# Graph attention kernel: edge steps of 128 instead of 256, softmax over 20 tiles instead of 16

## What is computed

```python
enh = xn + 0.1 * query_emb
Q, K, V = enh @ Wq + bq, enh @ Wk + bk, enh @ Wv + bv      # (N, 4 heads, 64)
mod_k  = K[src] + 0.2 * rel_w[edge_type]
scores = einsum('ehd,ehd->eh', Q[dst], mod_k) / 8
ex     = exp(scores - segment_max(scores, dst)[dst])
w      = ex / segment_sum(ex, dst)[dst]
agg    = segment_sum(w * V[src], dst)
out    = layernorm(agg @ Wo + bo + xn)                       # then the mix and the experts
```

## Time and profile before

| what | us |
|---|---|
| median of 3 runs (lowest, highest) | 1203.07 (1202.24, 1210.01) |
| the profiled execution, its own time | 1205.97 |
| span of its instructions | 1204.2 |
| busy, all stages: TensorE / VectorE / ScalarE / GpSimd | 1019.1 / 909.2 / 814.2 / 802.1 |

### The profile page before, as it was taken

One profiled execution on the slowest core, in us unless ns is written; L12 is line 12 of the kernel. 1 busy time (PEld: TensorE's weight loads), 2 busy tenths in 40 slices (PEclk: granted clock), 3 DMA queues, 4 the chain that ended last, 5 costly groups with the idle time before them and its releaser, 6 DMA issues. The chain is left out here.

```text
span 1204.2 us, 26894 instructions
## 1 busy us (share of the span) xinstructions
PE 1019.1 (85%) x6959; PEld 778.4 (65%) x6960; DVE 909.2 (76%) x1999; ACT 814.2 (68%) x2902; POOL 802.1 (67%) x873
## 2 busy tenths in 40 slices
PE   4899966888888888888888888878996489999993
PEld 3677744565565556555556565556895478999993
DVE  5777547999998999999999999985996823333331
ACT  3344410489888888898988889863675466766662
POOL 3667657777777777777777777712983347666662
PEclk9899975699998999999999999998997689999997
DMA  8333438888888888888888888876325724444445
GB/s 240 114 122 113 141 105 234 240 248 234 240 240 241 243 239 238 243 242 241 246 243 239 247 244 244 242 242 227 111 71 177 237 53 72 69 70 65 70 66 133
DMA packets 130432, 220.56 MB, mean 183 GB/s; under 512 B 24772, under 2 KB 89452, under 8 KB 129992
## 3 DMA queue, kind: packets, MB, share of 16 engines
q0 software_dynamic: 48832, 138.49, 42.9%
q1 hardware_dynamic: 81480, 80.63, 21.5%
HBM read 188.00 MB, written 34.25 MB: 185 GB/s over the span
## 5 line engine op out<-in xcount | busy, mean ns | idle before, releaser
L668 POOL DMA_INDIRECT KV<-kv,ixs x464 | 471.7, 1017 | 151.5 <-issue 110.9
L684 ACT ACTIVATE KV<-KV,WS 128x65 f32<-128x65 f32 x1728 | 437.2, 336 | 40.7 <-issue 40.6
L811 PE MATMUL ps_o<-KV,PM 128*128 128x260 f32 x928 | 255.5, 399 | 49.1 <-DVE PM L929 31.4
L785 PE MATMUL ps_qe<-Q,PT 128*128 x1392 | 209.6, 288 | 21.8 <-DVE PT L897 12.9
L811 PEld LDWEIGHTS ps_o<-KV,PM 128*128 128x128 f32 x928 | 160.4, 193 | 91.5 <-issue 73.0
L785 PEld LDWEIGHTS ps_qe<-Q,PT 128*128 128x128 bf16 x1392 | 122.4, 100 | 77.3 <-issue 46.5
L918 DVE TENSOR_TENSOR KV<-KV,ps_qe 128x512 f32<-128x512 f32 x232 | 149.5, 674 | 0.2
L911 DVE TENSOR_TENSOR KV<-KV,ps_u 128x1024 f32<-128x1024 f32 x116 | 140.0, 1207 | 12.8 <-DMA KV<-kv,ixs 12.5
L924 DVE TENSOR_REDUCE S<-KV 128x16 f32<-128x1024 f32 x116 | 138.7, 1196 | 1.1
L1705 DVE TENSOR_TENSOR YG<-ps_y,KV 128x256 f32<-128x256 f32 x56 | 23.8, 425 | 140.8 <-PE ps_y L1678 140.8
L1589 POOL DMA_INDIRECT acc<-YG,DX x56 | 88.7, 1583 | 61.3 <-issue 36.9
(11 more groups left out here) (306 smaller groups left out, 1610.5 us busy)
## 6 DMA issues: line engine op xcount, KB each, us to landing
dlb<-dl_rows SPq DMA_DIRECT2D x116, 128.0 KB
tyb<-ty_rows SPq DMA_DIRECT2D x116, 64.0 KB
KV<-kv,ixs POOLq DMA_INDIRECT x464
kv<-kvb SPq DMA_DIRECT2D x25, 258.0 KB, 2.5
xs_rows<-xs SPq DMA_DIRECT2D x25, 256.0 KB, 2.5
KV<-xs_rows SPq DMA_DIRECT2D x10, 640.0 KB, 9.8
Q<-in_f_W_dram SPq DMA_DIRECT2D x8, 512.0 KB, 6.0
KV<-in_f_W_dram SPq DMA_DIRECT2D x8, 512.0 KB, 6.0
```

The source lines that it names most:

```text
L668: pool.indirect_dma_start(kv[:, c % KR, n, :], None, d["kv"], bass.IndirectOffsetOnAxis(ap=T["ixs"][:, c % KR, n:n + 1], axis=0)).then_inc ...
L684: m = a.activation(part, part, ACT.Copy, scale=W[:, c % 2, s * H + h:s * H + h + 1])
L785: m = pe.matmul(T["ps_qe"][:, p % 3, k, :], T["PT"][:, h, (p % 2 * 2 + k) * P:(p % 2 * 2 + k + 1) * P], T["Q3"][:, bass.ds(at + n * C, C)] ...
L811: m = pe.matmul(ps_o[:, bass.ds(bank, A)], PM[:, p // 2 % 2, p % 2 * 2 + k, :], kv[:, c % KR, 2 * x + k, C:KVW], start=False, stop=True, s ...
```

## The change

Steps become one tile: `TE` = 128, ET = 416, 440 steps of one tile each. Chunks become 20 tiles, 5 groups: 22 chunks, 110 groups. The ring of gathered tiles is one ring of 48 tiles (`RING`), and the sums lag the scores by `LAG` = 9 groups; each engine has one loop over x = 0..118 (`NX` = 119). GpSimd reads its indices in `SRC` itself. Every tile now has its own clear and its own copy of the sums: TensorE loads 4 values instead of 2 in each of its three loads per group, ScalarE makes its two loads of 2 values twice per group. VectorE weighs the last tile of every odd group (`by_vector`), and in the last 9 groups three of four. In the projection the list of steps is made with 4 columns instead of 2 (4 gathers of edges instead of 2, 4 counts over 416 entries instead of 2 over 208). The areas of later stages within the ring are placed anew. The diff, cut:

```diff
-TE = 2 * P
+TE = P
-SC = 2
+SC = 4
-CP = 8
-NCH = NS // CP
-CG = 2 * CP // G
-CB_ = 2 * CP
-KR = 3
+CB_ = 20
+NCH = NS // CB_
+CG = CB_ // G
+NG = NS // G
+RING = 48
+LAG = 9
...
+    NX = NG + LAG
+    def by_vector(g):
+        if g >= NG - LAG:
+            return ((1, 1), (2, 2))
+        return ((3, 1),) if g % 2 else ()
...
-            sp.wait_ge(s_pw, (NCH - 2) * CP)
+            sp.wait_ge(s_pw, NS - RING + VB_TILES)
             sp.dma_start(T["VB"], d["kv"][:, C:KVW]...)
...
+            for t in range(NS):                                   # GpSimd
+                g = t // G
+                wait(pool, s_pw, t - RING + 1)
+                if t % G == 0:
+                    wait(pool, s_ku, g - AHEAD + 1)
+                pool.indirect_dma_start(kv[:, t % RING, :], None, d["kv"],
+                                        bass.IndirectOffsetOnAxis(ap=T["SRC"][:, t:t + 1], axis=0))...
...
+            for x in range(NX):                                   # ScalarE
+                c, j = x // CG - 1, x % CG
+                g = x - LAG
+                softmax, summed = 0 <= c < NCH, g >= 0
+                for k in range(G):
+                    t = g * G + k
+                    if summed:
+                        if k % 2 == 0:
+                            at, bank = before(max(t - 1, 0))
+                        if k in by_scalar(g):
+                            weigh(t)
+                        if t >= 2:
+                            copy_sums(t - 1, at[k % 2], bank[k % 2])
+                    if softmax and j == 1 and k == 1:
+                        ends(c)
+                if softmax and j == 2:
+                    exponents(c)
+                if softmax and j == 3:
+                    weights(c)
...
             def rows(G_):                                         # TensorE
-                return load_values(nc, mybir.EngineType.PE, T["qRow"][0:1, 2 * G_:2 * G_ + 2], (NT - 1) * 3 * C)
+                return load_values(nc, mybir.EngineType.PE, T["qRow"][0:1, G * G_:G * G_ + G], (NT - 1) * 3 * C)
...
+                if summed:
+                    own = banks("own_bank", g * G, G)
+                    after = banks("next_bank", max(g * G - 1, 0), G)
+                    shift = 1 if g == 0 else 0
+                def add(k):
+                    t = g * G + k
+                    if summed:
+                        if t >= 2:
+                            clear(t - 1, after[k - shift])
+                        aggregate(t, own[k])
...
+                if scored:
+                    queries(2 * G_, at[0:2])
+                add(0)
+                add(1)
+                if scored:
+                    relations(G_)
+                if softmax and j == 3:
+                    turn_weights(c)
+                if scored:
+                    queries(2 * G_ + 1, at[2:4])
+                add(2)
+                add(3)
...
+            for x in range(NX):                                   # VectorE, its new part of a step
+                if summed:
+                    for k, n in by_vector(g)[0 if scored else 1:]:
+                        weigh(g, k, n)
+                if scored:
+                    reduce(x)
```

More of the change, by code:

```diff
@@ L55 @@
 EARLY = 2
+VB_AT, VB_TILES = NS % RING, 13
 NSLOT = NTILE * SLOTS
@@ L694, in copy_sums @@
                 a.wait_ge(s_pw, q)
-                if q % CP == 0:
-                    a.wait_ge(s_rs, q // CP)
+                if q % CB_ == 0:
+                    a.wait_ge(s_rs, q // CB_)
                 wait(a, s_acc, q - 1)
                 a.copy(ACC[:, bass.ds(at, A)], ps_o[:, bass.ds(bank, A)]).then_inc(s_acc, 1)
-            def drain(i):
-                for g in range(CG):
-                    p = (i - 2) * CP + 2 * g
-                    softmax = i == NCH
-                    if softmax and g == 1:
-                        ends(i - 1)
-                    at, bank = before(p - 1)
-                    for k in range(2):
-                        copy_sums(p - 1 + k, at[k], bank[k])
-                        if softmax and g == 3 and k == 0:
-                            weights(i - 1)
-                    if softmax and g == 2:
-                        exponents(i - 1)
             def ends(c):
@@ L764, in _ @@
+            at, bank = before(NS - 2)
+            copy_sums(NS - 1, at[1], bank[1])
+            a.wait_ge(s_pw, NS)
+            a.wait_ge(s_acc, NS - 1)
             a.copy(ACC[:, NT * A:(NT + 1) * A], ps_o[:, (NT - 1) % RO * 512:(NT - 1) % RO * 512 + A]).then_inc(s_acc, 1)
@@ L1059, in _ @@
-            drain(NCH)
-            drain(NCH + 1)
+            for x in range(NX):
+                c, j = x // CG - 1, x % CG
+                g = x - LAG
+                softmax, summed, scored = 0 <= c < NCH, g >= 0, x < NG
+                if x + 1 < NG:
+                    onehots(x + 1)
+                if scored:
+                    modify(x)
+                if g > 0 and g % CG == 0:
+                    rescale(g // CG)
+                if summed:
+                    place(g)
+                if softmax and j == 2:
+                    carry_in(c, 0)
+                if scored:
+                    multiply(2 * x)
+                elif summed:
+                    weigh(g, *by_vector(g)[0])
+                if softmax and j == 2:
+                    carry_in(c, 1)
+                if scored:
+                    multiply(2 * x + 1)
+                if softmax and j == 0:
+                    run_forward(c)
+                if softmax and j == 1:
+                    carry(c)
+                if softmax and j == 2:
+                    differences(c)
+                if summed:
+                    for k, n in by_vector(g)[0 if scored else 1:]:
+                        weigh(g, k, n)
+                if scored:
+                    reduce(x)
+                if softmax and j == 0:
+                    run_backward(c)
+                if softmax and j == 1:
+                    carried(c)
```

359 lines of the change are left out of this document (118 added, 241 removed).

## The result

The kernel after takes 1231.24 us (median of 4 runs, 1230.29 to 1233.5) against 1202.65 for before beside it: ratio 1.0238, interval [1.0179, 1.0297]. The forecast was 1200.8. The profiled execution has a span of 1230.0, before's had 1204.2, a difference of 25.8 us.

| term | predicted | measured |
|---|---|---|
| first `modify` (start of the scored part) | -0.5 | +3.0 (187.83 against 184.80) |
| from there to the first sum | +5.0 | +3.3 |
| steady part, 101 groups against 108 | -22.3 (5.45 each) | +2.0 (574.8, 5.69 each) |
| drain | +15.5 (39.8) | +16.2 (40.4) |
| later stages | 0 | +1.3 |

A forecast was written before the change was run, and what follows sets the result against it. Four engines were taken to be within 0.4 us of one cadence, VectorE busiest before, ScalarE after. First sum of the drain 18.3 us earlier, drain +15.5, projection +0.5: -2.3 from 1203.07, so 1200.8 us; range 1184 to 1228.

The forecast's parts named there:

- steady part: Edge stage from first sum to drain: 101 groups at 5.45 us, against 108 at 5.30 before.
- drain: The last 9 groups, with ScalarE setting the pace: 39.8 us against 24.3 before, +15.5.
- rival C: TensorE's loads of four values make it the bound: step 6.7 us, +123 us, 1324 us; chance 0.13.
- half-way case: Within rival C: only next_bank's load, beginning one value off, is dear; claimed to leave TensorE where it was.
- I take SyncE's row: TensorE's loads of four values priced from SyncE's 298 ns: three loads a group fall from 1.63 to 0.9 us.
- TensorE then has room: TensorE in the edge stage: clears add 0.22 us a group, cheaper loads gain about 0.5, so it does not bind.
- The rule as a rival: The skill's 200 ns per register: a load of four some 0.9 us, making TensorE the bound; priced as rival C.
- ScalarE at 5.43: ScalarE's open loads and softmax give 27.15 us a chunk, 5.43 a group, passing VectorE by 0.09.
- VectorE's help does not shorten ScalarE's step: Edge stage, odd groups: loads lie open instead of the multiplications handed over; 5.20 us a group in any case.
- rival B: Late handovers between engines in the edge stage push the others: 5.60 us a group, +15.2, 1216.0 us; chance 0.19.
- The ring: Gathers wait for the sum of tile t - 48; each tile is free before its turn, so no cost.
- The projection: Stage before the edges, bound by TensorE: transposes +0.3 us, other work between 0 and +2; taken as +0.5.

The follow-up runs named there:

- e14: The kernel before, with TensorE's load of own_bank taken twice, 0.545 us more a group: 1206.74 us, ratio 1.0028.
- e1: The kernel after, with TensorE's next_bank row written one value later so its load of four begins on a multiple of four: 1205.48 us, ratio 1.0017.
- e12: e1 with own_bank loaded twice on TensorE, 0.33 us more a group: 1216.82 us, ratio 1.0111.
- e3: e1 with ScalarE's rows aRow and last_bank also shifted, each loaded as four values once a group: 1190.79 us, ratio 0.9877.
- e4: The kernel after, with no tile handed to VectorE in groups still scored: 1242.99 us, ratio 1.0311.
- e9: e3 with ScalarE's loads behind the first tile's multiplications and no tile to VectorE in groups still scored: 1181.92 us, ratio 0.9818.
- e8: The kernel after, with AHEAD = 2, so gathers come a group later: 1239.42 us, ratio 1.0276.
- e10: e3 with ScalarE's loads behind the first tile's multiplications, and qRow and aRow worked out in the projection's fifth tile: 1186.14 us, ratio 0.9862.
- e16: e9 with qRow and aRow worked out later, in the projection's fifth tile: 1179.29 us, ratio 0.9802.
- e11: e3 with ScalarE's loads behind the first tile's multiplications, plus 13 loads of own_bank on TensorE ahead of the edge stage: 1189.4 us, one execution.

## Why the prediction was wrong

**What bounds before.** That four engines are close to one cadence was right, and that TensorE had room; e14 filled it. By e14 the room was some 0.55 and not 0.37, since 0.18 of it was hidden in the busy time, so TensorE's own step was some 4.75 (an estimate, 5.30 - 0.55) and not 4.92. "... what the change gives to one counts at once" was the sentence to take seriously; the prediction then looked at ScalarE.

**The step that failed** is in rival C: "A half-way case, where only the load of `next_bank`, which begins one value off, is dear, leaves TensorE where it was." The case came: the loads are 1.66 us, as before 1.63. But TensorE was not left where it was. Its busy time is 409.5 us before and 406.5 after, but that is over 90.5 groups and over 84.4: 4.52 a group became 4.82, +0.29, where I had counted +0.22 for the clears. And the open part of the loads grew from 0.39 to 0.73, +0.34, where C had only +0.1 for "less is queued ahead of them". 4.91 + 0.29 + 0.34 = 5.55, and with the 0.13 of waits 5.68: the measured 5.69. This splits the measured step and does not prove it, since busy time is partly elastic (e14); what shows that TensorE's loads are the cause is e1, and e12 by its smaller dose.

The half-way case got a sentence and no sum. C's own terms would have made it 4.92 + 0.22 + 0.03 + 0.1 = 5.27, under ScalarE's 5.45, and so still harmless: the mis-sized term is the open part of the loads. And the rule by which an engine under the longest step costs nothing failed with it: by that count e12 should have stayed at 5.42, and it came to 5.53. The case stood in none of the chances. Two figures beside it are slips: by C's terms TensorE becomes the bound when a load of four takes 0.61, not 0.7, and 6.7 is 1.25 above 5.45, not 1.22.

**"I take SyncE's row".** Right for two loads of three (332 and 329 against 298), wrong for the third. "TensorE then has room" hung on it; e1 and e12 show that even with three cheap loads it has none, since 0.33 us more is felt. The Trainium skill's rule (Runtime: NRT & Kernel Launch, section Instruction fetch mechanics), about 200 ns for each register even in bulk, is near what was measured off the places that are multiples of four (0.24) and does not hold on them (330 ns for four). The page has the loads in mind that the runtime adds; those of this kernel read SBUF. The rule as a rival pointed to the right engine.

**ScalarE at 5.43.** The number was met once TensorE's row was mended (e1: 5.425, 1205.5 against my 1200.8), but not for my reason alone: taking ScalarE's open loads away (e1 to e3) brings 0.06 a group, not the 0.09 and more by which I let it lead, and TensorE is still felt in e1. That e1 met the number was partly luck.

**"VectorE's help does not shorten ScalarE's step".** Wrong by a quarter (e4); and with the loads covered the help brings nothing and seems to be a loss (e9).

**"... in my placing of the step each wait has 0.5 us or more to spare"**, the argument against rival B: wrong for the end of a chunk, where VectorE waits 1.19 us for the last sum. The case nearest to what came is B with 5.60 a group and 1216; its cause, though, is C's.

**The ring.** "So the wait costs nothing": right in the kernel after, but not because "each tile is free before its turn". GpSimd waited for it 112 times, 55 us in all; VectorE has no wait for gathers there because GpSimd had slack. e8 shows that there is no group of lead to give away.

**The drain.** 39.8 against 40.4, by the copies 0.56 and 1.20 apart that the earlier trace rows had shown. They stand in the trace of after (timeline of ScalarE):

```profile
839.10 0.38 ACT L708 COPY ACC<-ps_o  x1 [0.18 <-ACT ACC L708]
840.29 0.38 ACT L708 COPY ACC<-ps_o  x1 [0.82 <-PE ps_o L801]
840.85 0.38 ACT L708 COPY ACC<-ps_o  x1 [0.18 <-PE ps_o L801]
841.90 1.07 ACT L694 ACTIVATE KV<-KV,WS 128x65 f32<-128x65 f32 x4 [0.68 <-issue]
```

**The projection.** +0.5, "between 0 and +2", was too little: in the two profiles compared the one-hot of first rows starts 3.7 us later (183.42 against 179.74), and only its own shrinking brings the first `modify` to +3.0. I had set the row operations beside other work; they stand ahead of the second tile's evacuation, and moving them seems to give some 3 us back (e10, e16). The path is not shown.

## What to carry to other kernels

Look at where a register load begins as well as at how many values it takes: four values on a multiple of four cost one value's price, and a row kept one entry later turns "the tile before" into such a place. When several engines stand within a few tenths of the same step, work out the sum for every engine in every case, the half-way ones too, with its busy time and its open loads as separate terms, and give a step that ends 0.2 us under the longest a chance of its own; the engine that moves from waiting for others to idle for its own "issue" is the one to test, however low its busy share. The sign is no proof: e14 shows it too, at a cost of 3 us. And when a change comes out slower, mend its dearest single instruction before judging its idea: here the same steps of 128 edges are 2% slower with one row out of place and 2% faster with it in place and the rest tuned.

## What the runs showed of the hardware

- On TensorE a load of registers took 330 ns for four values on a multiple of four, 590 for eight, 1000 for four elsewhere, 1945 for eight from place 2, 540 to 563 for any two (e11). On ScalarE four values on their place took 307 ns (e3), where two took 488.
- TensorE's sequencer prepared matmuls that are addressed by registers hardly ahead of the engine (0.3 us in e5), so queued matmuls of this kind covered little of a load behind them (0.45 us by six of them).
- TensorE's busy time in a profile is not a fixed amount of work: the same matmuls were busy 4.52 us a group in the kernel before and 4.35 in e14, where the waits between them had gone.
- A load on an engine that has almost no room cost a share of its length, not all or nothing: 0.107 us a group for 0.33, 0.266 for 0.67. On the kernel before, where TensorE waited 0.38 a group, 0.55 more cost 3 us in 1200.
